# Last graph propagation: the counts' 32x32 squares turned on VectorE instead of on TensorE and in the DMA

## The reference, cut to what matters

```python
# L3, after a layer norm and a ReLU of x
norm = deg_inv_sqrt[row] * deg_inv_sqrt[col]        # row = src, col = dst, self loops added
msgs = label_mat[row] * norm[:, None]
out  = jax.ops.segment_sum(msgs, col, num_segments=num_nodes)
x    = x + out
```

## Time and profile before

| what | value |
|---|---|
| median of 3 runs | 9566.44 us (9564.32 to 9601.33) |
| span of the profiled execution, first to last instruction | 7616.9 us |
| mean granted TensorE clock, as a share of 2.4 GHz | 0.871 |
| instructions in the span | 269804 |
| the last propagation in the trace | about 6777 to 7617 us |

### The profile page before, as it was taken

One profiled execution on the slowest core, in us unless ns is written; L12 is line 12 of the kernel. 1 busy time (PEld: TensorE's weight loads), 2 busy tenths in 40 slices (PEclk: granted clock), 3 DMA queues, 4 the chain that ended last, 5 costly groups with the idle time before them and its releaser, 6 DMA issues.

```text
span 7616.9 us, 269804 instructions
## 1 busy us (share of the span) xinstructions
PE 6063.9 (80%) x100278; PEld 5357.0 (70%) x100279; DVE 4777.4 (63%) x7214; ACT 3977.9 (52%) x6952; POOL 4112.2 (54%) x4193
## 2 busy tenths in 40 slices
PE   5676666676766666777776599999999999999998
PEld 4555555555555555555554588888889999999998
DVE  5878777777777777778776899999940011110000
ACT  3666666666666666666665688888820000013333
POOL 2677777777777777777777388888810000000000
PEclk6878778777778778778787799999999999999999
DMA  7888888888888888888886699999998888889998
GB/s 192 255 257 265 249 265 250 266 252 262 257 256 263 250 266 250 266 250 267 249 266 215 197 316 317 317 315 317 318 278 267 262 284 277 278 237 201 198 201 167
DMA packets 1757738, 1964.21 MB, mean 258 GB/s; under 512 B 922685, under 2 KB 1422063, under 8 KB 1756735
## 3 DMA queue, kind: packets, MB, share of 16 engines
q1 hardware_dynamic: 1359632, 1349.47, 61.7%
q10 hardware_dynamic: 297478, 446.38, 18.0%
q0 software_dynamic: 100000, 158.60, 6.4%
HBM read 1258.29 MB, written 618.65 MB: 246 GB/s over the span
## 4 chain that ended last, share of the span: by engine, by line
PE 44%; issue 14%; DVE 14%; DMA 10%; ACT 8%; POOL 4%; ACTq 3%; SPq 2%; DVEq 1%; POOLq 0%
PE pG L2248 10%; PE pT L2131 6%; DMA cA<-stg 5%; ACT stg L2505 4%; PE pT L2248 3%; PE pG L2300 3%; POOL recB L1393 3%; PE pG L2287 3%; PE pR L2248 2%; PE pT L2135 2%; PE pG L2212 2%; DVE msum L1864 2%; DMA car<-cA 2%; DVE doh L1667 2%; DMA recB<-rec,qpos 1%
## 5 line engine op out<-in xcount | busy, mean ns | idle before, releaser
L1393 POOL DMA_INDIRECT recB<-rec,qpos x3125 | 3070.1, 982 | 1117.0 <-issue 851.2
L2131 PE MATMUL pT<-soh,doh 128*128 128x128 bf16 x10600 | 1634.5, 254 | 785.7 <-ACT stg L2505 738.7
L2505 ACT CAST stg<-pT 128x512 fp8e4<-128x512 f32 x2650 | 1473.7, 585 | 579.9 <-PE pT L2131 492.0
L2131 PEld LDWEIGHTS pT<-soh,doh 128*128 128x128 bf16 x10600 | 978.1, 112 | 957.9 <-ACT stg L2505 851.1
L2135 PE MATMUL pT<-car,qidb 128*128 128x256 fp8e4 x2597 | 859.4, 331 | 0.0
L2212 PE MATMUL pG<-mpl,doh 128*128 128x144 bf16 x10388 | 764.4, 227 | 31.7 <-POOL mpl L1418 23.1
L1667 DVE TENSOR_TENSOR doh<-dm,pG 128x2560 bf16<-128x2560 bf16 x530 | 782.0, 1476 | 2.0 <-ACT dm L2583 1.9
L1667 DVE TENSOR_TENSOR doh<-smd,pG 128x2560 bf16<-128x2560 bf16 x530 | 782.4, 1476 | 0.0
L1667 DVE TENSOR_TENSOR soh<-smd,pG 128x1280 bf16<-128x1280 bf16 x530 | 431.0, 813 | 444.1 <-ACT smd L2483 417.6
L2212 PEld LDWEIGHTS pG<-mpl,doh 128*128 128x128 bf16 x10388 | 666.8, 96 | 60.4 <-POOL mpl L1418 47.5
L1415 POOL TENSOR_TENSOR mpl<-mpl 128x480 f32<-128x480 f32 x530 | 523.6, 988 | 285.3 <-ACT mpl L2608 284.5
(11 more groups left out here) (275 smaller groups left out, 14951.5 us busy)
## 6 DMA issues: line engine op xcount, KB each, us to landing
recB<-zt ACTq DMA_DIRECT2D x102, 2425.5 KB
brec<-recB SPq DMA_DIRECT2D x477, 495.0 KB
erec<-recB SPq DMA_DIRECT2D x477, 495.0 KB, 5.5
cl<-cA SPq DMA_DIRECT2D x80, 2560.0 KB, 10.9
cA<-stg ACTq DMA_DIRECT2D x530, 320.0 KB
cl<-cA SPq DMA_DIRECT2D x40, 2720.0 KB, 11.3
drow<-dlD SPq DMA_DIRECT2D x157, 640.0 KB
srowB<-srD SPq DMA_DIRECT2D x265, 320.0 KB, 5.8
```

The lines of the kernel that those rows point to most:

```text
L1393: p.indirect_dma_start(recF, bass.IndirectOffsetOnAxis(ap=qpos[:, s, c:c + 1], axis=0), rec[:, s, c, :], None).then_inc(s_sc[s], 16)
L2131: ins = t.matmul(bank[:, h * 256 + b * 128:h * 256 + b * 128 + 128], doh[:, o, 2 * e + b, h * 128:(h + 1) * 128], soh[:, o, 2 * e + b, :], ...
L2505: a.copy(stg[:, o, :, e * 256:(e + 1) * 256], B8[6 + (g * 5 + e) % 2][:, :].rearrange("p (h x) -> p h x", h=2), saturate=False).then_inc(e ...
```

## The change

The last propagation is written anew; what stands before it is the same but for how `store_group` loads `xq`.

- The 49 blocks become 50 blocks of other sources: the partitions' four quadrants (32 each) hold 32 units of four different source groups. Quadrant q of set 0 belongs to group q, of set 1 to group 4 + q; set 2 has the halves of groups 8 and 9, with zeros where group 9 is short. `xq` is loaded back from `hS` to match (`units`).
- The counts are loaded plainly with the destinations on the partitions, 32 at a time: `xi[32q + r, f, c]` is the row of destination 32 f + r of this turn's 256, group J's units along c. It is four transfers for a set (`fill`): SP issues those of quadrants 0 and 1, ScalarE those of quadrants 2 and 3.
- One VectorE instruction for a set (`v.transpose`, STREAM_TRANSPOSE in the listings) turns every 32x32 square of two-byte units in its quadrant, from `xi` to `yt`: 5120 units on each partition for sets 0 and 1, 2560 for set 2.
- There are 49 turns of 256 destinations (2 windows), each with three sets: 80 + 80 + 40 matmuls. A turn uses one PSUM bank.
- TensorE's flips, ScalarE's copies and the turning transfers are gone. Buffers are double (`i % 2`) for each set.
- The sum of a turn is one reduction of 288 values and two `scalar_tensor_tensor` of 48.

```diff
+        def fill(eng, half, i, s):
+            if i >= 2:
+                eng.wait_ge(z_tr, nth(i - 2, s))
+            for h in range(2):
+                q = half * 2 + h
+                if s < 2:
+                    place, J, c0, w = xi[i % 2][s][32 * q:32 * q + 32, :, :], 4 * s + q, 0, GB * 64
+                else:
+                    J, w = (8, 320) if half == 0 else (9, 256)
+                    place, c0 = xi[i % 2][2][32 * q:32 * q + 32, :, 0:w], h * w
+                eng.dma_start(place, cA[J, i * 256:(i + 1) * 256, c0:c0 + w].rearrange("(f r) c -> r f c", r=32)
+                              ).then_inc(l_x[i % 2][s], 16)
...
+                def transposed(i, s):
+                    v.wait_ge(l_x[i % 2][s], (i // 2 + 1) * 64)
+                    if i >= 2:
+                        v.wait_ge(z_rd, nth(i - 2, s))
+                    elif s == 2:
+                        v.wait_ge(z_ms, 2)
+                    v.transpose(ytu[i % 2][s], xiu[i % 2][s]).then_inc(z_tr, 1)
...
-                    gathered(r, JG - 1, 1, NB - (JG - 1) * GB)
+                    if r == 1:
+                        v.wait_ge(y_rd, 2 * JG * 6 - 1)
+                        transposed(0, 0)
+                        transposed(0, 1)
+                    gathered(r, JG - 1, 1, NB - (JG - 1) * GB, (lambda: transposed(1, 0)) if r else None)
+                def summed_up(i):
+                    o = i % 2
+                    v.wait_ge(z_rd, nth(i, 2))
+                    if i >= 2:
+                        v.wait_ge(z_ad, 2 * (i - 1))
+                    v.tensor_reduce(ysC[:, o, 0:2, :], B8[o][:, 0:6 * D].rearrange("p (w k d) -> p w d k", w=2, k=3),
+                                    AX.X, ALU.add).then_inc(z_ev, 1)
+                    v.wait_ge(z_ev, i + 1)
+                    for w in range(2):
+                        j = 2 * i + w
+                        v.scalar_tensor_tensor(out=qx3[:, j, :], in0=ysC[:, o, w, :], scalar=qdi[:, j:j + 1],
+                                               in1=qx3[:, j, :], op0=ALU.mult, op1=ALU.add).then_inc(z_ad, 1)
+                v.wait_ge(s_ht, (JG - 1) * 16)
+                transposed(1, 1)
+                transposed(0, 2)
+                transposed(1, 2)
+                for i in range(2, NTURN):
+                    transposed(i, 0)
+                    transposed(i, 1)
+                    summed_up(i - 2)
+                    transposed(i, 2)
+                summed_up(NTURN - 2)
+                summed_up(NTURN - 1)
...
-                def flip(i, o, n, nw):
...
-                def handing(i, o, nw, after_, known):
...
+                def product(i, s):
+                    o = i % 2
+                    t.wait_ge(z_tr, nth(i, s))
+                    if s == 0 and i >= 2:
+                        t.wait_ge(z_ev, i - 1)
...
+                    for n in range(SETS[s]):
+                        for b in range(UB):
+                            for w in range(2):
+                                ins = t.matmul(B8[o][:, w * 3 * D:(w + 1) * 3 * D],
+                                               ytf[o][s][:, n, w * 128:(w + 1) * 128, b], xq[:, FIRST[s] + n, b, :],
...
-                def flipped(i, o, nw, after_, known):
...
+                def store_out(g):
+                    a.wait_ge(z_ad, 8 * g + 8)
...
+                for i in range(3, NTURN):
+                    for s in range(3):
+                        fill(a, 1, i, s)
+                    if i >= 8 and i % 4 == 0:
+                        store_out(i // 4 - 2)
...
-                def load_turned(i, n, nw, first):
...
+                for i in range(2, NTURN):
+                    for s in range(3):
+                        fill(sp, 0, i, s)
```

More of the change, by code:

```diff
@@ L40 @@
 CZ = 12288
+UB = 2
+UNIT = BF16
 ER = 125
@@ L1251, in tidied @@
             return r * (AD[0] * JG) + J * AD[r]
[L1253 to L1262, removed]
         def rowed(K, g):
@@ L2313, in _ @@
+                t.wait_ge(y_ev, settled(1, JG - 1))
+                t.wait_ge(l_xw, 8 * 16)
+                for i in range(2):
+                    for s in range(2):
+                        product(i, s)
+                for i in range(2):
+                    product(i, 2)
+                for i in range(2, NTURN):
+                    for s in range(3):
+                        product(i, s)
         @block.scalar
@@ new lines, in store_group @@
+                    if J < 8:
+                        units(J % 4, FIRST[J // 4], J * GB * 128, 40 // UB)
+                    else:
+                        w = (20 if J == 8 else 16) // UB
+                        for h in range(2):
+                            units((J - 8) * 2 + h, FIRST[2], J * GB * 128 + h * w * 32 * UB, w)
+                def store_out(g):
+                    a.wait_ge(z_ad, 8 * g + 8)
+                    a.dma_start(out[g * 1024:(g + 1) * 1024, :].rearrange("(j p) d -> p j d", p=128),
+                                qx3[:, g * 8:(g + 1) * 8, :]).then_inc(s_qo, 16)
@@ new lines, in _ @@
+                for J in range(JG - 1):
+                    store_group(J, GB)
+                a.wait_ge(y_rd, 2 * JG * 6 - 2)
+                fill(a, 1, 0, 0)
+                fill(a, 1, 0, 1)
+                a.wait_ge(y_rd, 2 * JG * 6)
+                for i, s in ((1, 0), (1, 1), (0, 2), (1, 2)):
+                    fill(a, 1, i, s)
+                store_group(JG - 1, NB - (JG - 1) * GB, lambda: fill(a, 1, 2, 0))
+                fill(a, 1, 2, 1)
+                fill(a, 1, 2, 2)
+                for i in range(3, NTURN):
+                    for s in range(3):
+                        fill(a, 1, i, s)
+                    if i >= 8 and i % 4 == 0:
+                        store_out(i // 4 - 2)
@@ L2911, in _ @@
-                hold(sp, y_rd, 2 * JG * 6 - 2)
-                load_turn(0, WN, True)
-                load_turn(1, WN)
-                with sp.Fori(2, 12) as i:
-                    load_turn(i, WN)
-                load_turn(12, 2)
+                sp.wait_ge(y_rd, 2 * JG * 6 - 2)
+                fill(sp, 0, 0, 0)
+                fill(sp, 0, 0, 1)
+                sp.wait_ge(y_rd, 2 * JG * 6)
+                for i, s in ((1, 0), (1, 1), (0, 2), (1, 2)):
+                    fill(sp, 0, i, s)
```

164 lines of the change are left out of this document (61 added, 103 removed).

## The result

In the first comparison the changed kernel took 9476.44 us in the median (9430.65 to 9479.62, 4 runs), the one before 9566.2: a ratio of 0.9885, 95% interval 0.9859 to 0.991, 90 us less. The forecast was 9450 within 9340 to 9570, with 0.78 on faster. On another chip, where both kernels are some 1950 us quicker, the same two took 7499.78 and 7621.89 us: 0.984 (0.9826 to 0.9853), 122 us less; on a third 9405.26 and 9507.85: 0.9884 (0.9868 to 0.9901), 103 us less.

The account below looks back on a forecast made before the run. TensorE bounded the kernel before; VectorE was to bound the changed one. Start to 6807 us, 47 turns (686), 3.7 and 3.5 us gave 7500, 117 less than 7616.9, so 9449 us, forecast as 9450, range 9340 to 9570.

Parts of the forecast that it names:

- VectorE becomes the bound at 14.6 us a turn: Last propagation: transposes, reduction and two small instructions take VectorE 14.6 us a turn, against 12.5 for TensorE.
- the f32 rows: Earlier profile's f32 tensor_tensor timings, 1.04 ns an element plus about 158 ns, used to put the 5120-unit transpose at 5.5 us.
- the overlap: VectorE instructions following each other without a wait overlap by some 0.08 us, taking a turn from 14.8 to 14.6 us.
- The sum for the last propagation: Start until 6807 us, 47 turns of 14.6 us (686), then 3.7 and 3.5 us, ending at 7500.
- The tail: After the last transpose: 3.7 us of remaining TensorE matmuls, then 3.5 us from the last reduction to the span's end.
- The 1949.5 us outside the span: Part of a run's time taken to lie outside the recorded span and to stay unchanged: 1949.5 us.
- Loads at nothing: Count loads of the last propagation, 3.21 MB a turn at 220 GB/s, were taken to cost no time.
- Rivals 2 and 3: Slow count loads set the pace: 189 GB/s giving 9550 us (chance 0.10), or 161 GB/s giving 9695 (0.08).
- rival 3: Transfers to low and high partitions don't run together: 161 GB/s, +129 us, 9695 us; chance 0.08.
- Rival 1: Transposes at 0.52 ns a unit, VectorE's turn 7.7 us, TensorE stays the bound: -221 us, 9345 us; chance 0.12.
- rival 4: Transposes at 2.08 ns a unit, 10.7 us for 5120: +500 us and more, near 10060 us; chance 0.05.
- Rival 5: TensorE at 0.7 to 0.8 of full clock, 16.2 us a turn: -32 us, no change; chance 0.04.

Follow-up runs that it names:

- e3: The changed kernel with four-byte instead of two-byte units, so half the units per transpose: 7406.78 us, ratio 0.9713 to the kernel before.
- e1: The kernel before, run again unchanged for a profile: median 7620.8 us with a span of 7618.1 us, ratio 0.9997.
- e11: The changed kernel with four-byte units and all count loads issued by SP, none by ScalarE: 9389.11 us in one run.
- e8: The changed kernel with half of the products left out from turn 2 on: 9377.57 us in one run, last propagation 715.6 us.
- e6: The changed kernel with four-byte units, SP loading quadrants 0 and 2, ScalarE 1 and 3: 9312.87 us, ratio 0.9803 to the kernel before.
- e7: The changed kernel with four-byte units and half of the products left out from turn 2 on: 9285.11 us in one run.
- e2: The changed kernel again, no edit, on a quick chip: 7499.78 us, ratio 0.984 to the kernel before.

## Why the prediction was right, point by point

- **VectorE becomes the bound at 14.6 us a turn.** Right: 14.37. The transpose of 5120 was put at 5.5 us by the f32 rows and takes 5.47; 2560 take 2.84 (2.8). The 0.2 us too much are in the overlap: the six durations add up to 14.7 us (14.8 forecast), and the turn is 0.36 us shorter than that, where I took off 0.2. e3 adds what the rows could not say: the pace is one unit, not one byte pair, in 1.03 to 1.08 ns. The estimate from the Trainium skill ("Vector Engine (DVE) Microarchitecture Reference", section 3.8, with the clock of "VectorE: DVE Perf Modes") was 5.3 us; the trace agrees within 3%.
- **The sum for the last propagation.** 723 us were forecast (7500 less 6777), 720 measured. By terms: the start to the end of transpose (1,2) 30 us, measured 31.7 (8784.4 less 8752.7); 47 turns 686, measured 675.2; tail 3.7 + 3.5, measured 9.7 + 3.3. That the sum is within 3 us is partly luck: the turns were 11 us too long and the start and the end together 7.5 too short.
- **The tail, mis-sized.** I had TensorE follow each transpose. It cannot: turn i uses the bank of turn i-2, whose sum stands on VectorE behind transposes (i,0) and (i,1). So TensorE starts a turn only after that sum (46 waits for ysC, 81.4 us in all) and then runs its 200 matmuls in one piece. So the 2 us a turn that I expected it to wait for `yt` are a wait for `ysC`. That is free while TensorE has slack, and costs 6 us at the end.
- **The 1949.5 us outside the span.** Wrong, as e1 shows: a run's time is its span and 2 us, and the profile came from a quick execution. The difference of times survives this since I left that number the same for both kernels; but that it came out near the measured median of slow runs rests on the last propagation being the same on all chips, which I had not asked. 117 us were forecast, and 90, 103 and 122 measured, the last on the chip where the first part holds still.
- **Loads at nothing.** Right for this kernel's turns (one wait, before the first transpose), but with less room than I said: a DMA share of 0.91 at 227 GB/s where I had 0.7 to 0.85. The 60 ns a packet were right; the count was not, as some 3500 packets go in a turn, with the small ones of the result stores among them, where I counted the loads' 3072. The one wait costs a little: the first transpose starts 5.4 us before the last dense matmul and not 8, and the start is 1.7 us longer than forecast.
- **Rivals 2 and 3** (slow loads) had the size wrong. A single queue brings 229 GB/s (e11), too little for TensorE's turn of 12.5 us but above the 186 GB/s from which rival 3 would have made the kernel slower. The rule of the Trainium skill beside them ("SBUF — State Buffer", "Can I just issue two DMAs to hit both halves?") says that two transfers to the two halves gain 6% over one. No run here sets one transfer against two. The nearest are streams of transfers: 18% more from two queues that write both halves than from one queue (271 against 229 GB/s), and 7% more than from two that write the same half (253). The 200 GB/s estimated from it are below what one queue brings.
- **Rival 1** (0.52 ns a unit) and **rival 4** (2.08) fall with the 5.47 us. **Rival 5**, the clock, falls with the 1.00 of the middle. e8's 0.75 cost nothing, but with half of the matmuls; with all of them a clock of 0.77 would have made TensorE's turn 16.2 us, above VectorE's 14.4.

## What to carry to other kernels

Moving work to an idle engine is worth the old bound less the new engine's own turn, so the sum has to be made for that engine to the end: here 240 us that could be won became 120 us of gain, mostly since VectorE needs 14.4 us a turn where TensorE needs 12.5 (88 us in 47 turns). If an operation's time goes by elements and only bytes are moved, make the elements wider first, where neighbours may stay together: this doubled the transposes' pace and brought another 87 us. When a PSUM bank is reused, find where the instruction that frees it stands in the other engine's program; its place, not its length, decides when the next turn may begin.

## What the runs showed of the hardware

- The transpose of 32x32 squares: 5.47 us for 5120 two-byte units on 128 partitions, 2.84 for 2560 of two bytes and 2.85 for 2560 of four. No faster pace for two-byte data, as bf16 tensor_tensor has in the earlier trace rows.
- Loads of 32 partitions in packets of 1280, 640 and 512 B, all traffic of the middle counted: 229 GB/s from one queue (e11), 253 from two that write the same half of the partitions (e6), 271 from two that write different halves (e7), with slices of up to 327 there. What limits each is not separated from the issuing engine.
- The same first part of the kernel takes 5564 to 5576 us on a quick chip and 7441 to 7540 on the others. From 1000 to 5000 us of the changed kernel, first on a slow chip (the first comparison) and then on the quick one (e2), TensorE's costliest group is the same instruction with other waits:

```profile
L2187 PE MATMUL pT<-soh,doh 128*128 128x128 bf16 x6941 | 1274.0, 283 | 834.2 <-ACT stg L2542 587.1 <-issue 238.3
```

```profile
L2187 PE MATMUL pT<-soh,doh 128*128 128x128 bf16 x8460 | 1307.5, 255 | 650.2 <-ACT stg L2542 612.4 <-issue 0.2
```

On the slow one TensorE waits 238.3 us before this group for nothing that the profile shows ("issue"), 0.9 us at a time in the mean, against 0.2 us in all on the quick one, and its clock is 0.65 there against 0.83. VectorE's and ScalarE's durations are the same within 1% (1477 and 1475 ns for the `doh` instruction, 585 and 586 for the `stg` cast), GpSimd's within 2% (965 and 984). What holds the instructions back on these chips stays open; no run was made for it.
